# One-hots of a table lookup: one VectorE instruction of two broadcast inputs in place of eight compares with a scalar per partition

## The reference

```python
e = jnp.stack([tbl_0[ids[:, 0]], ..., tbl_25[ids[:, 25]]], axis=1)          # 26 embeddings of 128 per sample
combined = jnp.concatenate([dense_features[:, None, :], e], axis=1)         # 27 features of 128
interactions = jnp.einsum('bfd,bgd->bfg', combined, combined)[:, TRIU_I, TRIU_J]   # 351 pairs
z = jnp.concatenate([dense_features, interactions, dense_features], axis=1)
h = jnp.maximum(z @ W_top1 + b_top1, 0.0)      # 512
h = jnp.maximum(h @ W_top2 + b_top2, 0.0)      # 256
y = h @ W_top3                                 # 1
```

## Time and profile before

| | us |
|---|---|
| median of 3 runs | 382.09 (381.57 to 382.64) |
| the profiled execution | 381.72 |
| its span | 379.9 |
| PE busy | 348.5 |
| VectorE busy | 245.8 |
| ACT busy | 129.8 |
| POOL busy | 265.2 |

### The profile page before, as it was taken

How to read it: one execution, slowest core, us unless ns; L and a number is a source line. 1 busy time by engine, 2 the same in 40 slices (tenths; PEclk the granted TensorE clock), 3 DMA queues, 4 the chain that set the end, 5 groups by cost and what they waited for, 6 DMA issues and landing times.

```text
span 379.9 us, 14079 instructions
## 1 busy us (share of the span) xinstructions
PE 348.5 (92%) x6148; PEld 313.3 (82%) x6148; DVE 245.8 (65%) x777; ACT 129.8 (34%) x287; POOL 265.2 (70%) x263
## 2 busy tenths in 40 slices
PE   1776689999999999999999999999999999988877
PEld 1665679998989899898989899898989899877676
DVE  4999979876558856586557856597467755521111
ACT  3445225334314234134314234233324233232221
POOL 6777777777778777787778777787778777782000
PEclk9999999999999999999999999999999999998999
DMA  7768922242123212132123222232121212110000
GB/s 267 221 197 261 315 68 55 55 126 58 49 59 112 60 51 56 52 119 57 51 59 108 65 54 54 59 112 57 50 59 30 58 51 57 52 48 25 2 4 2
DMA packets 13951, 31.29 MB, mean 82 GB/s; under 512 B 5177, under 2 KB 6850, under 8 KB 13890
## 3 DMA queue, kind: packets, MB, share of 16 engines
q0 software_dynamic: 8192, 16.79, 16.6%
q1 hardware_dynamic: 5698, 13.60, 10.7%
HBM read 30.36 MB, written 0.01 MB: 80 GB/s over the span
## 4 chain that ended last, share of the span: by engine, by line
PE 83%; DVE 12%; issue 3%; DMA 1%; ACT 0%; SPq 0%; DVEq 0%
PE p_hot L298 36%; PE pgram L312 14%; PE ph L345 14%; DVE onehot L491 9%; PE pmix L356 7%; PE p_fetch L286 6%; DVE table_sb L481 3%; PE pmix L364 2%; PE pmix L327 1%; DMA ids<-ids_hot 1%; PE pgram L391 1%; PE p_hot L345 0%; PE p_hot L381 0%; ACT h L610 0%; DVE y_sb L477 0%
## 5 line engine op out<-in xcount | busy, mean ns | idle before, releaser
L266 POOL DMA_INDIRECT emb<-tbl,ids_sb x256 | 264.4, 1033 | 79.1 <-issue 76.8
L491 DVE TENSOR_SCALAR onehot<-ids,row_of 128x256 fp32r<-128x256 int16 x640 | 197.4, 380 | 67.8 <-PE p_hot L298 63.0
L298 PE MATMUL p_hot<-onehot,table_sb 128*128 128x256 f32 x1280 | 175.4, 291 | 19.3 <-DVE onehot L491 16.4
L298 PEld LDWEIGHTS p_hot<-onehot,table_sb 128*128 128x128 f32 x1280 | 159.6, 193 | 27.5 <-issue 13.7
L560 ACT ACTIVATE xt<-p_hot 128x256 f32<-128x256 f32 x80 | 52.2, 652 | 169.9 <-PE p_hot L298 168.5
L312 PE MATMUL pgram<-xt 128*32 128x26 f32 x4096 | 56.8, 195 | 8.4 <-issue 5.1
L312 PEld LDWEIGHTS pgram<-xt 128*32 128x32 f32 x4096 | 46.5, 109 | 21.0 <-issue 18.3
L560 ACT ACTIVATE xt<-p_fetch 128x512 f32<-128x512 f32 x64 | 45.7, 714 | 2.9 <-PE p_fetch L286 2.9
L345 PE MATMUL ph<-late,w_sb 128*128 128x256 f32 (+1 forms) x180 | 44.0, 382 | 0.6 <-ACT h L610 0.6
L286 PE MATMUL p_fetch<-ident,emb 128*128 128x128 f32 x256 | 38.4, 273 | 0.0
L345 PEld LDWEIGHTS ph<-late,w_sb 128*128 128x128 f32 x180 | 33.3, 195 | 4.7 <-issue 0.8
(11 more groups left out here) (47 smaller groups left out, 84.3 us busy)
## 6 DMA issues: line engine op xcount, KB each, us to landing
ids<-ids_hot SPq DMA_DIRECT2D x8, 640.0 KB, 3.9
late<-tbl SPq DMA_DIRECT2D x10, 512.0 KB, 3.9
emb<-tbl,ids_sb POOLq DMA_INDIRECT x256
dense_sb<-dense_t SPq DMA_DIRECT2D x8, 128.0 KB, 3.9
w_sb<-w1p SPq DMA_DIRECT2D x1, 768.0 KB, 7.6
w_sb<-w SPq DMA_DIRECT2D x1, 512.0 KB, 7.9
w_sb<-w1a SPq DMA_DIRECT2D x1, 256.0 KB, 6.6
h<-w1b SPq DMA_DIRECT2D x1, 256.0 KB, 7.0
```

The lines of the kernel that those rows point to most:

```text
L266: pool.indirect_dma_start(out=emb[:, i % PLACES, n, :], out_offset=None, in_=tables[f], in_offset=bass.IndirectOffsetOnAxis(ap=ids_sb[:, t ...
L298: last = pe.matmul(p_hot[:, at % 2, 0:WIDE], table_sb[:, table, part, v, :], onehot[:, at % RING, v, :], start=(part == 0 and v == 0), sto ...
L491: last = dve.tensor_scalar(onehot[:, at % RING, v, :], ids_16[:, k % 2, table, :], row_of[:, v:v + 1], None, ALU.is_equal)
```

## The change

The eight compares of a one-hot, each of 256 ids with one scalar per partition, become one two-input compare over 8 x 256 elements. Its first input is the row of 256 ids, read again for each chunk (a step of 0 over the chunks); the second is `row_of`, each of its eight numbers repeated 256 times (a step of 0 over the samples). `row_of` becomes int16, so both inputs are. The output, its place and its type stay, as do the wait in front and the semaphore behind.

```diff
-        row_of = sb("row_of", [P, VC])
+        row_of = sb("row_of", [P, VC], I16)
...
                 wait(dve, s_looked, at - RING + 1)
-                for v in range(VC):
-                    last = dve.tensor_scalar(onehot[:, at % RING, v, :], ids_16[:, k % 2, table, :], row_of[:, v:v + 1],
-                                             None, ALU.is_equal)
-                last.then_inc(s_hot, 1)
+                dve.tensor_tensor(onehot[:, at % RING, :, :], ids_16[:, k % 2, table, :].unsqueeze(1).to_broadcast([P, VC, WIDE]),
+                                  row_of[:].unsqueeze(2).to_broadcast([P, VC, WIDE]), ALU.is_equal).then_inc(s_hot, 1)
```

## The result

The changed kernel takes 478.93 us (median of 5 runs, 476.48 to 479.27) where the kernel before takes 382.09: a ratio of 1.2546, 95% interval 1.2507 to 1.2586. The forecast was 379.8 us, faster, with a range up to 384.5. The profiled execution spans 474.7 us for 379.9.

What follows compares the result with a forecast made beforehand. PE was taken to bound the kernel, with VectorE's one-hots on the path in the first 48 us and at 57.76. -2.8 - 0.3 + 0.8 = -2.3 us on 381.72 gave 379.4, for the median 379.8 us; range 378.0 to 384.5.

Steps and rivals of the forecast that it cites:

- part four: POOL's gathers: shorter 4.93 us gathers gain nothing, since PE has some 17 gathers, 21 us, in hand; counted as no change.
- The rival on the gathers: The new instruction shuts gathers out for its whole length, POOL bounds, over 100 us slower in all; chance 0.04.
- The duration: One new two-input one-hot instruction of 2048 elements on VectorE lasts 2.33 us.
- the step: Time from one new one-hot instruction on VectorE to the next instruction: 2.26 us, against 2.56 for eight compares.
- The rival by which the steps of 0 are slow: Repeats or zero steps make VectorE's new instruction step over 2.37 us, so the kernel gets slower; chance 0.16.
- The start: First 48 us, where PE waits for one-hots: shorter one-hots let PE start its steady work 2.8 us earlier.
- The wait at 57.76: PE's one wait for one-hots in the long middle stretch goes away: -0.3 us.
- The tight places: Six places behind the copy of y, where one-hots come 0.11 to 0.14 us late for PE: +0.8 us.
- No gather of 4.9 us: Sign that the prediction holds: POOL's long gathers during runs of compares are gone.
- gathers off their 1.25 us beat: Sign on POOL that would make the prediction wrong: gathers no longer start every 1.25 us.
- no change: Case with the one-hot stepping 2.33 to 2.45 us on VectorE: time 381.0 to 383.2 us; chance 0.13.
- h: The time VectorE steps per new one-hot instruction, taken as 2.26 us; each 0.1 us more costs 2.1 us in all.

Runs made afterwards that it cites:

- e11d: The kernel before with its first 12 one-hots as two two-input instructions of 1024 elements each, compares for the rest: ratio 1.0118 to the kernel before.
- e2: The kernel after with POOL's gathers left out, each group of four rows one plain load of fixed rows issued by ACT: 372.77 us.
- e5b: The kernel after with the compare reading two dense float32 table rows from the second pair of tiles on: 562.6 us beside 613.95 for the kernel before.
- e9b: The kernel after with one instruction of one tensor input and one scalar per one-hot: 571.77 us beside 613.95 for the kernel before.
- e3: The kernel after with each one-hot as two two-input instructions of 1024 elements instead of one of 2048: 429.68 us.
- e9c: Repeat of the kernel after with one instruction of one tensor input and one scalar per one-hot: 581.3 us beside 614.28 for the kernel before.
- e7b: The one instruction for the five odd tables, the kernel before's eight compares for the five even ones: 540.85 us beside 613.95 for the kernel before.

## Why the prediction was wrong

The step that failed is part four, "at nothing": "POOL loses one 4.93 us gather in each pair for one of 0.94. PE has some 17 gathers in hand". The gather of 4.93 us did not go, it became 5.56 us (151.22), and the others, which I took for unmoved, are held 1.56 us per one-hot. The 17 in hand cover 21 us once; 101 us more of holding than before pass them by. The rival on the gathers named this mechanism and its size, "over 100 us slower in all", and got a chance of 0.04.

That chance rested on one reading: L481 is a two-input instruction, it starts level with a gather, and the beat of 1.25 us goes on the earlier trace rows. The reading was right and the conclusion was not. An L481 lasts 1.27 us, and it began 0.01 us before a gather: the next gather begins only as it ends. And a gather that starts together with the instruction is not held: in the kernel after, too, the gather of 170.96, 0.03 us into a one-hot, lasts 0.94 us, and that of 293.21, 0.10 us into one, 3.01. That ten L481 in the trace of before held no gather was no set of ten independent samples: the cycle of L481 and eight compares was 3.745 us, three beats of 1.248, so all L481 stood at the same place of the beat, within 0.03 us. In the kernel after the cycle is another, an L481 falls elsewhere, and the gather of 16.06 is held by it. The cost of one hold, with the 2.29 and 0.82 us of the traces of after: a gather that begins u us into an instruction of 2.29 is late by 2.29 + 0.82 - 0.94 - u = 2.17 - u, 1.55 in the mean over a beat of 1.25, and ten of these are 15.5 us per pair of tiles where POOL had some 3 to spare (43.3 less 32 x 1.25). 40 + 15.5 = 55.5 us a pair; the gathers of the kernel after take 443 / 8 = 55.4. My price for this rival, holding POOL for the full length of each, was above it: 22.6.

The other points, one by one:
- The duration, 2.33 us forecast, 2.29 measured, and the step, 2.26 forecast, some 2.20 (two in 4.49): right, and equal for dense inputs. The rival by which the steps of 0 are slow falls. The Trainium skill's figure for a read that hops at every element (Vector Engine (DVE) Microarchitecture Reference, section Measured stream behaviour on trn2), 1.73 ns per column, does not apply to a step of 0: 2288 ns for 2048 elements is 1.12 ns each with the fixed part.
- The start, -2.8: not seen. PE's last wait there for a one-hot ends at 46.07 in the kernel after, for 45.58 before, and PE has by then waited for gathered rows, 4.17 us until 32.18. The chain of e11d also meets late rows, at 37.17.
- The wait at 57.76, -0.3: not to be seen, PE waits for rows there.
- The tight places, +0.8: right in kind and near in size at the one read in e2, 0.09 for 0.11 and 0.10 for 0.14.
- "No gather of 4.9 us" among the signs: wrong; "gathers off their 1.25 us beat" was the sign that the prediction is wrong, and it came.
- The bounds of "no change" do not follow from the price of 2.1 us per 0.1 us of h: 0.07 and 0.19 over 2.26 would be 381.3 and 383.8, not 381.0 and 383.2. Nothing hangs on it.
- The rule of the Trainium skill (SBUF — State Buffer, section Who interferes with whom and the text on the shared pair): I weighed it as if the gathers did not read SBUF. A gather takes its row numbers from `ids_sb`, which lies in SBUF. The traces agree with the rule once the gather's early point is taken for that read; that it is the read was not shown by a run.

## What to carry to other kernels

Before many short VectorE instructions are merged into one long one, with two inputs in SBUF or with one input at two elements a step, look for indirect DMAs on POOL's queue: here one that began inside such an instruction stood still until it ended, so a merge that frees VectorE can make POOL the bound. Count the time held per instruction (about its length less the mean place in the beat) against what POOL has to spare per cycle. Before a row is read as "these two don't disturb each other", check whether all its repeats stand in the same phase of one another; ten locked repeats are one. Smaller pieces of the same instruction held less here (1.56 us per one-hot whole, 0.97 in halves, 0.98 in eighths), but never as little as the compares with a scalar (24 us over 80, 0.30).

## What the runs showed of the hardware that I had not expected

A gather begun 0.10 us or more inside a long VectorE instruction, and over 0.13 us before its end, ends 0.81 to 0.83 us after it: with two inputs (all 77 gathers over 1.1 us of the kernel after, all 75 of e5b) and with one input at two elements a step (29 in e9b). The latter also stops a gather that began 0.19 to 0.44 us before it, which then ends 0.12 after; the two-input form leaves such a gather at 0.94 to 0.95 (three in the kernel after, begun 0.23 to 0.39 us before it). The hold is given up between two back-to-back instructions in most places (e3, 102.92) and not in some behind an L477 copy, where one gather lasted through 32 instructions, 11.6 us.

In four series of runs, on four chips, the kernel before took 595 to 622 us. No trace of it was kept there; the kernel of e11d, the same but for the first 12 one-hots, took about as long, and its PE stood idle 149.5 us in front of the matmuls of the products of pairs (L315), for 8.4 in the first trace of the kernel before (L312). It stops after a few matmuls while gathers run, and not where POOL pauses: in e11d 51 follow in one go from 109.90, while no gather runs from 108.91 to 114.72. The timeline of e9c near 45 us, and in its tail, where POOL is done:

```profile
44.80 0.32 PE L312 MATMUL pgram<-xt 128*32 128x26 f32 x5 [0.42 <-issue]
45.51 0.34 PE L312 MATMUL pgram<-xt 128*32 128x26 f32 x5 [0.40 <-issue]
...
539.83 1.50 PE L312 MATMUL pgram<-xt 128*32 128x26 f32 x154
```

There the kernels that hold the gathers off through the whole batch were the faster ones (e5b 562.6, e7b 540.85 beside 613.95), though not in the order of the time held (133 and 66 us). What puts an execution into this condition stays open; one chip showed both.
